# Expert outputs scattered to a row per token and choice, and read back by plain transfers

## The chip, the cores and the metric

One core of a Trainium2 chip. TensorE (PE) multiplies and transposes, VectorE (DVE) and ScalarE (ACT) read its results, GpSimd (POOL) does elementwise work and issues indirect transfers, SyncE (SP) issues the plain ones. Every engine runs its own list of instructions in order. The metric is the time of one execution in microseconds, median of several; lower is better.

## The reference

Input x is 64 x 64 x 128 (4096 tokens of 128 floats). Six residual layers follow: a gated delta rule, self and cross attention with their feed-forward parts, a block of attention and a mixture of experts, a causal attention, a mixture over eight ensembles, and a last mixture of experts. The change concerns the two mixtures in which each token goes to its two best experts of eight. Cut to what matters (the first is called f here, the last g):

```python
logits = tok @ gate_w.T + gate_b                      # f; g has no bias
topv, topi = jax.lax.top_k(softmax(logits), 2)
topv = topv / jnp.sum(topv, axis=-1, keepdims=True)
combine = zeros.at[arange(n_tok)[:, None], topi].set(topv)
for e in range(8):
    h = relu(tok @ w1[e].T + b1[e]) @ w2[e].T + b2[e]
    moe_out = moe_out + combine[:, e:e + 1] * h
x = layernorm(tok + moe_out)                          # f only; g adds moe_out to x
```

## The kernel before

The tokens are held as 16 groups of 256. A first phase ("one") does the first three layers group by group and is not touched. The second phase ("last") does the rest. In it four programs per engine (slots 0 to 3, each with a quarter of the groups and of the tiles) are woven into one list by a written string of digits, `ORDER["last"][engine]`: each digit says which program goes on to its next `yield`. Further digits stand for side programs: on POOL 4 and 5 are the `posts`, 6 to 9 the fetches; on SP 0 to 3 load expert weights, 4 to 7 store results, 8 and above do the rest. A `wait_ge` on a semaphore stops its whole engine, since the list is in order.

A mixture of experts goes like this, once for f and once for g, in two halves of tokens (f: 16 and 16 columns of 128 tokens, g: 20 and 12):

- `dve_route` and `pe_inv` sort the (token, choice) pairs by expert into tiles of 128 rows. There is room for 78 tiles in f and 78 in g (32 columns x 2 choices = 64 full tiles, and 7 more per half, since each expert's last tile may be part empty). Their results are POS (for each token and choice: its row among the tiles), EID (each tile's expert) and INV (each tile's 128 tokens), the last written in line 1994 after a copy in line 1992.
- `pool_fetch` gathers a tile's 128 rows of 512 bytes by an indirect transfer (line 2011), four buffers per slot.
- `pe_tiles` turns the tile, multiplies it by the first expert matrix (line 2122) and, after ScalarE's relu (line 2157), by the second (line 2143). `dve_tiles` adds the bias into one of two buffers wy of the slot (line 2180, signal `t_y`).
- `sp_stores` stores wy as it is, tile after tile, by a plain transfer to `yf` or `ys` in HBM (line 2095, signal `l_y`). wy is free again when that store has landed.
- `pool_got`, called by `pool_post0` (f) and `pool_post1` (g), waits until the last eight tiles of all that it reads have landed, then gathers for a group of 256 tokens the two results of each: four indirect transfers of 128 rows (line 1750) into one of two buffers GOT. `dve_two` adds them to the tokens, four instructions (line 1728, signal `q_two`), and GOT is free for the group after the next.
- In f a norm follows (`dve_post0`, POOL lines 651, 1777 and 1779, signal `q_x`) and then the causal attention, the ensembles and g's gate (`attn1`, `xattn1`, `pre1`), whose programs need POOL in lines 651 (power), 1514 (masked keys) and 2240. In g the result is stored (`sp_out`, line 2338) and the program ends.

Between f and the causal attention the tokens change their layout; `sp_back` reads the tokens, gates and positions back from HBM in the new one, and POSb holds the positions. The table WX serves f's second matrices, and then the ensembles: line 2326 loads it anew after f's last tile.

## Time and profile before

| | |
|---|---|
| time, median of 3 (lowest to highest) | 2222.42 us (2219.38 to 2223.92) |
| the profiled execution | 2224.8 us, its span 2222.9 us |
| PE, DVE, ACT, POOL busy | 86%, 70%, 55%, 43% of the span |
| f's tiles | about 1290 to 1555 us |
| attention, ensembles, g's gate | about 1555 to 2015 us |
| g's tiles | about 1995 to 2183 us |
| end | 2183 to 2222.9 us |

The span is from the first to the last instruction. "Idle before" is how long an engine stood still before the instructions of a group, and the name behind the arrow is what it waited for last. "Issue" means that it waited for nothing that the profile shows.

### The profile page before, as it was taken

To read this page: it belongs to the slowest core of one execution; us is meant where nothing else is said; L and a number is where in the kernel's file an instruction comes from. 1 tells how busy PE (TensorE), PEld (TensorE's weight loads), DVE (VectorE), ACT (ScalarE), POOL (GpSimd) and SP (SyncE) were. 2 spreads that over 40 slices of the span, in tenths; PEclk is the share of its full clock that TensorE was granted. 3 is DMA by queue.
4 is the path that set the end of the run, shared out by engine and by line. 5 is a ranking of instruction groups with operands and counts; after the bars stand their busy time and mean duration, and the time that the engine had idled before them with its cause. 6 is when DMAs were issued, how large, how long until landed. Compare 5 with 4: busy or idle time off the path is not lost.

```text
span 2222.9 us, 67944 instructions
## 1 busy us (share of the span) xinstructions
PE 1911.7 (86%) x27216; PEld 1571.6 (71%) x27216; DVE 1554.9 (70%) x4301; ACT 1211.9 (55%) x2811; POOL 961.7 (43%) x1176
## 2 busy tenths in 40 slices
PE   6789888989988998899979689787598999899992
PEld 4666676767767776677757478677377888789991
DVE  7488678787878877789757844684588766865332
ACT  6356775577765785557756345243244554344551
POOL 3542336423354234542244454250777422125466
PEclk9999999999999999999999799999599999999996
DMA  4000000000000000000010044577111010006883
GB/s 147 5 6 2 1 2 6 6 1 2 2 6 5 2 2 2 5 5 2 1 39 9 13 115 111 148 191 187 61 30 29 9 46 4 9 16 189 236 227 112
DMA packets 98342, 110.71 MB, mean 50 GB/s; under 512 B 32048, under 2 KB 72496, under 8 KB 97520
## 3 DMA queue, kind: packets, MB, share of 16 engines
q1 hardware_dynamic: 88944, 87.73, 14.1%
q0 software_dynamic: 9088, 18.63, 3.4%
q8 instruction: 221, 3.62, 0.7%
q14 instruction: 89, 0.73, 0.1%
HBM read 89.73 MB, written 16.58 MB: 48 GB/s over the span
## 4 chain that ended last, share of the span: by engine, by line
PE 58%; DVE 18%; ACT 9%; issue 7%; POOL 6%; DMA 2%; SPq 0%; POOLq 0%; DVEq 0%; ACTq 0%
PE PS L2143 6%; PE PS L2122 5%; PE PS L685 4%; PE PS L1592 4%; PE PS L1598 4%; PE PS L1071 3%; POOL GOT L1750 3%; PE PS L1086 2%; PE PS L1047 2%; DVE mx L1065 2%; PE PS L1171 2%; PE PS L1188 2%; PE PS L1060 2%; PE PS L1078 2%; PE PS L1150 2%
## 5 line engine op out<-in xcount | busy, mean ns | idle before, releaser
L2157 ACT ACTIVATE wh<-PS,we 128x128 f32<-128x128 f32 x624 | 173.3, 380 | 198.9 <-PE PS L2122 198.5
L2011 POOL DMA_INDIRECT wx<-x,INV x156 | 153.2, 982 | 150.8 <-PE PS L2134 54.6
L651 POOL TENSOR_TENSOR xrs<-xrs,Cs 128x2 f32<-128x2 f32 x112 | 78.9, 704 | 318.5 <-DVE xrs L643 317.3
L1065 DVE TENSOR_REDUCE mx<-PS 128x8 f32<-128x512 f32 x256 | 175.1, 684 | 57.1 <-PE PS L1047 28.6
L2122 PE MATMUL PS<-wxT,we 128*128 128x128 f32 x1248 | 168.9, 282 | 18.6 <-issue 14.6
L1067 DVE TENSOR_TENSOR P<-PS,mx 128x512 f32<-128x512 f32 x256 | 177.1, 692 | 8.8
L1514 POOL TENSOR_TENSOR km<-qk,Cs 128x1024 f32<-128x1024 f32 x64 | 121.2, 1901 | 129.9 <-ACT qk L1471 56.1
L1071 PE MATMUL PS<-Cs,P 128*128 128x128 f32 x1024 | 156.0, 284 | 18.7 <-ACT P L1229 12.4
L2122 PEld LDWEIGHTS PS<-wxT,we 128*128 128x128 f32 x1248 | 154.7, 196 | 24.0 <-issue 22.4
L1628 ACT ACTIVATE eh<-PS 128x256 f32<-128x256 f32 x256 | 93.6, 383 | 134.1 <-PE PS L1592 132.5
L1592 PE MATMUL PS<-exF,WX 128*128 128x256 f32 x512 | 150.5, 395 | 10.8 <-DVE X L1648 6.4
L1071 PEld LDWEIGHTS PS<-Cs,P 128*128 128x128 f32 x1024 | 117.8, 144 | 47.6 <-ACT P L1229 19.9
L1598 PE MATMUL PS<-WX,eh 128*128 128x128 f32 x1024 | 134.2, 276 | 0.1
L1598 PEld LDWEIGHTS PS<-WX,eh 128*128 128x128 f32 x1024 | 129.3, 192 | 7.1 <-ACT eh L1628 2.3
L629 ACT ACT_TABLE_LOAD x99 | 127.0, 1283 | 1.8
L1017 POOL TENSOR_TENSOR ET<-AT,Cs 128x512 f32<-128x512 f32 x64 | 83.3, 1306 | 93.0 <-PE PS L685 92.9
L2143 PE MATMUL PS<-WX,wh 128*128 x624 | 96.9, 295 | 22.6 <-DVE wxT L2175 17.7
L2180 DVE TENSOR_TENSOR wy<-PS,we 128x128 f32<-128x128 f32 x156 | 43.0, 288 | 96.2 <-PE PS L2143 84.3
L1648 DVE SCALAR_TENSOR_TENSOR X<-PS,ggt,X 128x128 f32<-128x128 f32 x256 | 76.7, 345 | 46.2 <-PE PS L1598 45.4
L1202 ACT ACTIVATE km<-PS,Cs 128x256 f32<-128x256 f32 x256 | 108.0, 483 | 0.0
L2143 PEld LDWEIGHTS PS<-WX,wh 128*128 128x128 f32 x624 | 83.4, 202 | 30.2 <-issue 29.5
L1487 ACT ACTIVATE P<-P 128x512 f32<-128x512 f32 x128 | 78.7, 629 | 46.9 <-DVE P L1067 46.0
(356 smaller groups left out, 5132.0 us busy)
## 6 DMA issues: line engine op xcount, KB each, us to landing
we<-in_wf SPq DMA_DIRECT2D x78, 322.0 KB, 4.2
we<-in_wl SPq DMA_DIRECT2D x78, 322.0 KB, 4.0
yf<-wy SPq DMA_DIRECT2D x78, 64.0 KB
ys<-wy SPq DMA_DIRECT2D x78, 64.0 KB
R<-in_wa SPq DMA_DIRECT2D x1, 3072.0 KB, 15.5
wx<-x,INV POOLq DMA_INDIRECT x156, 3.6
X<-in_x SPq DMA_DIRECT2D x4, 512.0 KB, 15.2
WX<-in_wf SPq DMA_DIRECT2D x1, 2048.0 KB, 7.8
```

The costliest lines, as they stand in the source:

```text
L629: e.preload_act_table_set(name)
L1065: e.tensor_reduce(A.mx[r], S3, AX, ALU.max).then_inc(*o.inc())
L1067: return e.tensor_tensor(v3(dst, NA), S3, bc(A.mx[r], 2, 64), ALU.subtract)
L1071: i = e.transpose(dst[:, 128 * k:128 * k + 128], P[:, 128 * k:128 * k + 128], ID)
L1202: i = e.activation(km[:, :, j, :], v3(ps(s, r)[:, W:2 * W], NB), ACT.Copy, scale=c("m64", j, j + 1))
L1514: e.tensor_tensor(A.km.rearrange("p (b j t) -> p b j t", b=NB, j=4), bc(v3(A.qk[:, W:2 * W], NB), 2, 4), bc(bc(c("m8", 4 * h, 4 * h + 4), ...
L1592: e.matmul(o, w1[:, x_, 128 * f:128 * f + 128], B.xF, True, True).then_inc(*sig.inc(G, "h_up", x_, f))
L1598: i = e.matmul(o[:, 128 * t:128 * t + 128], h[:, W * f + 128 * t:W * f + 128 * t + 128], w2[:, x_, f, :], f == 0, f == 1)
L2011: e.indirect_dma_start(out=WB[s].x[q // NS % NX], out_offset=None, in_=x1[k], in_offset=bass.IndirectOffsetOnAxis(ap=INV[k % NH][:, q - T0 ...
L2122: i = e.matmul(ps(s, 1)[:, 128 * f:128 * f + 128], w[:, 128 * f:128 * f + 128], B.xT, True, True)
L2143: i = e.matmul(ps(s, 0)[:, 0:128], B.h[:, 128 * f:128 * f + 128], W2[y][:, bass.ds(w2 + 128 * f, 128)], f == 0, f == 3)
L2157: i = e.activation(B.h[:, 128 * f:128 * f + 128], ps(s, 1)[:, 128 * f:128 * f + 128], ACT.Relu, bias=w[:, 512 + f:513 + f])
```

## The change

Results go to HBM already in token order, so that reading them back needs no index:

- `pool_got`, `pool_post1` and `sp_stores` go. New on POOL is `pool_scatter`, four programs (digits a to d): each tile is put by one indirect transfer to the rows of its tokens and choices. Rows of a tile that hold no token get a number beyond the table, and are left out by the bounds check.
- New on SP is `sp_got`: each group of 256 tokens is read by one plain transfer (128 partitions, two pieces of 1 KB each) into GOT. The number of GOT buffers (2) and wy buffers (2 per slot) stays.
- The destination rows DST come from `dve_route`. The second product of `pe_inv` now carries the pair's number, not the token column's; before INV stand four reads of PSUM and four short instructions, where one copy stood, and after it five more for DST (f: six), in the signal `r_dst`.
- POSb goes, and the positions are no longer sent through HBM (PG holds gates only).
- All five strings of the second phase are written anew. Its steps and their work are the same otherwise.

```diff
-            "4447944555755544449447555555444444555555444444555555444444555555444444555555444444555555",
+            "a69d9b6a6dcad7bb69acd7da886b8ca7dc88c7cb7c9dcb8a7b69a7966ba77a8dd9b9db9ad9b9c89dc7a9c6ddbb66ddccababdada",
...
-        def pool_got(e, s, G, y):
...
-            for q in range(T0[last + 1] - 2 * NS, T0[last + 1]):
-                e.wait_ge(*l_y.landed(q))
...
-                    e.indirect_dma_start(out=GOT[G % 2][:, t, k, :], out_offset=None, in_=rows,
-                                         in_offset=bass.IndirectOffsetOnAxis(ap=at, axis=0)).then_inc(*l_got.inc(G))
...
             e.wait_ge(*sig.at(k, "r_inv"))
-            e.tensor_copy(R.idf, ps(0, 1)[:, 0:TILES]).then_inc(*o.inc())
-            e.wait_ge(*o.now())
-            e.scalar_tensor_tensor(out=inv, in0=ps(0, 1)[:, TILES:2 * TILES], scalar=128.0, in1=R.idf, op0=ALU.mult, op1=ALU.add).then_inc(*sig.inc(k, "r_tok"))
+            part_, nth = ps(0, 1)[:, 0:TILES], ps(0, 1)[:, TILES:2 * TILES]
+            e.tensor_scalar(R.ji, nth, 1.0, 0.0, ALU.subtract, ALU.max)
+            e.tensor_scalar(R.jf, nth, 1.0, 0.0, ALU.subtract, ALU.max)
+            e.tensor_copy(R.idf, part_)
+            e.tensor_scalar(R.em, nth, 0.5, float(2 ** 20), ALU.is_lt, ALU.mult).then_inc(*o.inc())
...
+            e.tensor_scalar(R.oi, R.ji, 1, None, ALU.bitwise_and).then_inc(*o.inc())
...
+            e.tensor_copy(R.of, R.oi).then_inc(*o.inc())
...
+            e.tensor_tensor(R.to, R.jf, R.of, ALU.subtract).then_inc(*o.inc())
...
+            e.scalar_tensor_tensor(out=inv, in0=R.to, scalar=64.0, in1=R.idf, op0=ALU.mult, op1=ALU.add).then_inc(*sig.inc(k, "r_tok"))
...
+        def pool_scatter(e, s):
+            yield
+            for y in "fg":
+                for n_, q in enumerate(tiles_of(s, y)):
+                    k = part(q)
+                    to = yf if y == "f" else ys[k % NH]
+                    e.wait_ge(*sig.at(k, "r_dst"))
+                    e.wait_ge(*sig.at(q, "t_y"))
+                    e.indirect_dma_start(out=to, out_offset=bass.IndirectOffsetOnAxis(ap=DST[k % NH][:, q - T0[k]:q - T0[k] + 1], axis=0), in_=WB[s].y[n_ % 2],
+                                         in_offset=None, bounds_check=int(to.shape[0]) - 1, oob_is_err=False).then_inc(*l_y.inc(q))
+                    yield
...
-        def sp_stores(e, s):
+        def sp_got(e):
             yield
             for y in "fg":
-                for n_, q in enumerate(tiles_of(s, y)):
-                    e.wait_ge(*sig.at(q, "t_y"))
-                    rows = ys[part(q) % NH][place(q), :] if y == "g" else yf[128 * q:128 * q + 128, :]
-                    e.dma_start(rows, WB[s].y[n_ % 2]).then_inc(*l_y.inc(q))
+                for G in range(NG):
+                    h = half_with(G, y)
+                    first = groups_of(h, y)[0] if y == "g" else 0
+                    if G == first:
+                        last = 1 if y == "f" else NH + h
+                        for q in range(T0[last + 1] - 2 * NS, T0[last + 1]):
+                            e.wait_ge(*l_y.landed(q))
+                    if G >= 2:
+                        e.wait_ge(*sig.at(G - 2, "q_two", y))
+                    elif y == "g":
+                        e.wait_ge(*sig.at(NG - 2 + G, "q_two", "f"))
+                    rows = (yf if y == "f" else ys[h]).rearrange("(t p k) d -> p t (k d)", p=128, k=2)
+                    t = NT * (G - first)
+                    e.dma_start(GOT[G % 2].rearrange("p t k d -> p t (k d)"), rows[:, t:t + NT, :]).then_inc(*l_got.inc(G))
                     yield
```

The lists show three places. First, POOL when g's tiles begin, before (line 2011 is the fetch of a tile, wx its buffer; `tiles_dve_2` is the signal that slot 2 has a result):

```order
L2011 DMA wx_1_515<-x,INV_66 128x128 [waits route_dve_0,turned_pe_1]
L651 TENSOR_TENSOR ers_481<-ers_481,Cs 128x2 [waits two_dve_1]
L651 TENSOR_TENSOR ers_495<-ers_495,Cs 128x2 [waits two_dve_3]
L2011 DMA wx_2_523<-x,INV_66 128x128 [waits route_dve_0,turned_pe_2]
L2011 DMA wx_2_524<-x,INV_66 128x128 [waits route_dve_0,turned_pe_2]
L2011 DMA wx_3_533<-x,INV_66 128x128 [waits route_dve_0,turned_pe_3]
L2011 DMA wx_2_525<-x,INV_66 128x128 [waits route_dve_0,turned_pe_2]
L2011 DMA wx_0_504<-x,INV_66 128x128 [waits route_dve_0,turned_pe_0]
```

and after (line 2003 is the fetch, line 2017 the scatter of a result wy):

```order
L2003 DMA wx_1_540<-x,INV_68 128x128 [waits route_dve_0,turned_pe_1]
L651 TENSOR_TENSOR ers_506<-ers_506,Cs 128x2 [waits two_dve_1]
L2017 DMA ys<-wy_2_553,DST_66 5120x128 [waits tiles_dve_2,route_dve_0]
L2003 DMA wx_0_529<-x,INV_68 128x128 [waits route_dve_0,turned_pe_0]
L2017 DMA ys<-wy_2_554,DST_66 5120x128 [waits tiles_dve_2,route_dve_0]
L2003 DMA wx_0_530<-x,INV_68 128x128 [waits route_dve_0,turned_pe_0]
L651 TENSOR_TENSOR ers_520<-ers_520,Cs 128x2 [waits two_dve_3]
L2003 DMA wx_2_547<-x,INV_68 128x128 [waits route_dve_0,turned_pe_2]
```

Scatters stand between the fetches, each waiting for its slot's result. Behind the row of ers_520 follow 137 rows to the end of the list, all of them fetches or scatters; from g's first fetch to the end there are 158 rows: 156 indirect transfers and the two power rows.

Second, POOL near the end of its list, before (the last gathers of g's first half, POS_60, and the first of its second, POS_61, four for each group, after the tiles' results have landed, `l_y`):

```order
L1750 DMA GOT_384<-ys,POS_60 128x128 [waits l_y2,l_y1,l_y3,l_y0,l_y4,l_y7,post1_dve_0,l_y6,l_y5]
L1750 DMA GOT_384<-ys,POS_60 128x128 x3
L1750 DMA GOT_385<-ys,POS_60 128x128 [waits l_y2,l_y1,l_y3,l_y0,l_y4,l_y7,post1_dve_1,l_y6,l_y5]
L1750 DMA GOT_385<-ys,POS_60 128x128 x3
L1750 DMA GOT_384<-ys,POS_61 128x128 [waits l_y1,l_y0,l_y2,l_y7,l_y3,l_y6,post1_dve_0,l_y5,l_y4]
L1750 DMA GOT_384<-ys,POS_61 128x128 x3
L1750 DMA GOT_385<-ys,POS_61 128x128 [waits l_y1,l_y0,l_y2,l_y7,l_y3,l_y6,post1_dve_1,l_y5,l_y4]
L1750 DMA GOT_385<-ys,POS_61 128x128 x3
```

and after (fetches into wx, scatters from wy):

```order
L2017 DMA ys<-wy_1_543,DST_67 3072x128 [waits tiles_dve_1,route_dve_0]
L2003 DMA wx_0_528<-x,INV_69 128x128 [waits route_dve_0,turned_pe_0]
L2003 DMA wx_0_529<-x,INV_69 128x128 [waits route_dve_0,turned_pe_0]
L2017 DMA ys<-wy_3_563,DST_67 3072x128 [waits tiles_dve_3,route_dve_0]
L2017 DMA ys<-wy_3_564,DST_67 3072x128 [waits tiles_dve_3,route_dve_0]
L2017 DMA ys<-wy_2_553,DST_67 3072x128 [waits tiles_dve_2,route_dve_0]
L2017 DMA ys<-wy_2_554,DST_67 3072x128 [waits tiles_dve_2,route_dve_0]
L2017 DMA ys<-wy_0_534,DST_67 3072x128 [waits tiles_dve_0,route_dve_0]
L2017 DMA ys<-wy_1_544,DST_67 3072x128 [waits tiles_dve_1,route_dve_0]
L2017 DMA ys<-wy_0_533,DST_67 3072x128 [waits tiles_dve_0,route_dve_0]
```

Five more scatters end the list. The 24 gathers of g's last six groups are gone from it, and six reads on SP stand in their place.

Third, SP when f's tiles end, before (line 2095 stores a result, line 2326 loads the ensembles' table):

```order
L2095 DMA yf<-wy_3_538 128x128 [waits tiles_dve_3]
L2095 DMA yf<-wy_1_519 128x128 [waits tiles_dve_1]
L2095 DMA yf<-wy_2_528 128x128 [waits tiles_dve_2]
L2095 DMA yf<-wy_0_509 128x128 [waits tiles_dve_0]
L2326 DMA WX<-in_wx 128x4096 [waits tiles_pe_0,tiles_pe_1,tiles_pe_3,tiles_pe_2]
L2063 DMA x<-gzq_540 128x2x128 [waits two_dve_0]
L2063 DMA x<-gzq_541 128x2x128 [waits two_dve_1]
```

and after (line 2109 reads a group's results, `post0_dve` is the signal of `dve_two` and the steps behind it):

```order
L2109 DMA GOT_409<-yf 128x2x256 [waits l_y2,l_y3,l_y1,l_y4,l_y0,l_y5,l_y7,l_y6]
L2109 DMA GOT_410<-yf 128x2x256
L2109 DMA GOT_409<-yf 128x2x256 [waits post0_dve_0]
L2109 DMA GOT_410<-yf 128x2x256 [waits post0_dve_1]
L2109 DMA GOT_409<-yf 128x2x256 [waits post0_dve_0]
L2109 DMA GOT_410<-yf 128x2x256 [waits post0_dve_1]
L2336 DMA WX<-in_wx 128x4096 [waits tiles_pe_0,tiles_pe_1,tiles_pe_3,tiles_pe_2]
```

The stores have moved to POOL; the table's load, which came right after them, now comes behind the reads of six groups, the last two of which wait for groups 2 and 3 to be added.

## Rows read from the trace of the kernel before

**Rows 1.** The page: busy time, share of the span and instructions of each engine.

```profile
PE 1911.7 (86%) x27216; PEld 1571.6 (71%) x27216; DVE 1554.9 (70%) x4301; ACT 1211.9 (55%) x2811; POOL 961.7 (43%) x1176
```

**Rows 2.** Windows: us; PE, PEld, DVE, ACT, POOL busy; granted clock; DMA share; GB/s.

```profile
1445.00:1555.00 110.00, 90.11 (x695) 84.54 (x695) 73.15 (x129) 46.30 (x168) 38.22 (x38) 0.94 0.79 190
1555.00:1575.00 20.00, 0.00 (x0) 0.00 (x0) 7.43 (x28) 0.00 (x0) 13.98 (x16) 0.54 0.41 142
1575.00:1610.00 35.00, 28.06 (x246) 17.41 (x246) 23.96 (x60) 12.60 (x25) 27.98 (x26) 0.53 0.06 16
1610.00:1750.00 140.00, 128.14 (x1332) 105.12 (x1329) 119.12 (x387) 63.36 (x157) 103.98 (x111) 1.00 0.10 27
...
1995.00:2183.00 188.00, 176.41 (x1505) 169.69 (x1502) 74.24 (x284) 92.39 (x330) 113.45 (x118) 1.00 0.75 209
2183.00:2222.90 39.90, 0.00 (x0) 0.00 (x0) 9.66 (x32) 0.00 (x0) 25.00 (x27) 0.52 0.31 85
```

**Rows 3.** Chain that ended last, 1540 to 1760 us: shares by line.

```profile
by line: POOL GOT L1750 18.2%; issue 11.9%; PE PS L1592 6.5%; PE PS L1598 5.8%; DVE X L1728 5.1%; PE PS L1060 3.9%; PE PS L1071 3.7%; PE PS L1086 3.6%; PE PS L2143 2.8%; POOL X L1777 2.7%; POOL km L1514 2.6%; DVE X L647 2.5%; PE PS L2122 2.
```

**Rows 4.** Timeline of POOL as f's results are read: start, us, instruction, idle before.

```profile
1557.25 0.95 POOL L1750 DMA_INDIRECT GOT<-yf,POSb  x1 [50.17 <-DMA yf<-wy]
```

**Rows 5.** Timeline of DVE there.

```profile
1552.46 0.88 DVE L2180 TENSOR_TENSOR wy<-PS,we 128x128 f32<-128x128 f32 x4 [5.26 <-PE PS L2143]
1563.74 1.27 DVE L1728 SCALAR_TENSOR_TENSOR X<-GOT,PGb,X 128x128 f32<-128x128 f32 x4 [10.40 <-DMA GOT<-yf,POSb]
...
1568.77 2.10 DVE L1728 SCALAR_TENSOR_TENSOR X<-GOT,PGb,X 128x128 f32<-128x128 f32 x4 [0.29 <-DMA GOT<-yf,POSb]
...
1581.68 1.25 DVE L1728 SCALAR_TENSOR_TENSOR X<-GOT,PGb,X 128x128 f32<-128x128 f32 x4
...
1591.19 1.26 DVE L1728 SCALAR_TENSOR_TENSOR X<-GOT,PGb,X 128x128 f32<-128x128 f32 x4
...
1617.10 1.27 DVE L1728 SCALAR_TENSOR_TENSOR X<-GOT,PGb,X 128x128 f32<-128x128 f32 x4
```

**Rows 6.** Timeline of POOL at the end.

```profile
2213.72 0.95 POOL L1750 DMA_INDIRECT GOT<-ys,POS  x1 [0.30 <-issue]
2214.98 0.95 POOL L1750 DMA_INDIRECT GOT<-ys,POS  x1 [0.30 <-issue]
```

**Rows 7.** Timeline of DVE at the end: last result, last two groups added.

```profile
2179.95 0.29 DVE L2180 TENSOR_TENSOR wy<-PS,we 128x128 f32<-128x128 f32 x1 [0.52 <-PE PS L2143]
...
2212.47 1.26 DVE L1728 SCALAR_TENSOR_TENSOR X<-GOT,GK,X 128x128 f32<-128x128 f32 x4 [3.75 <-DMA GOT<-ys,POS]
2217.51 1.26 DVE L1728 SCALAR_TENSOR_TENSOR X<-GOT,GK,X 128x128 f32<-128x128 f32 x4 [3.78 <-DMA GOT<-ys,POS]
```

**Rows 8.** DMA issues of the page: KB each, median us from issue to landing.

```profile
we<-in_wf SPq DMA_DIRECT2D x78, 322.0 KB, 4.2
...
x<-X SPq DMA_DIRECT2D x16, 128.0 KB, 1.8
...
WX<-in_wx SPq DMA_DIRECT2D x1, 2048.0 KB, 8.1
```

**Rows 9.** Line 1592, the ensembles' first product: ns, first and last start us.

```profile
L1592 PE MATMUL PS<-exF,WX x512: 379/379/483, 1623.7 to 2015.2; 128*128 128x256 f32 x171
```

**Rows 10.** Timeline of DVE as INV of g's first half is written.

```profile
1995.94 0.21 DVE L1992 COPY ridfk<-PS 128x47 f32<-128x47 f32 x1 [2.64 <-PE PS L1860]
1996.19 0.21 DVE L1994 SCALAR_TENSOR_TENSOR INV<-PS,ridfk 128x47 int32<-128x47 f32 x1
```

**Rows 11.** Timeline of POOL where g's fetches begin.

```profile
1997.16 1.05 POOL L2011 DMA_INDIRECT wx<-x,INV  x1 [5.53 <-DVE INV L1994]
1998.51 0.95 POOL L2011 DMA_INDIRECT wx<-x,INV  x1 [0.30 <-issue]
```

**Rows 12.** Line 2095, the stores: ns min/median/max to issue one, first and last start us.

```profile
L2095 SPq DMA_DIRECT2D ys<-wy x78: 319/432/1314, 2007.8 to 2180.3; - x78
```

**Rows 13.** Tile wx: ns min/median/max, first and last start us; issue to landing.

```profile
L2011 POOL DMA_INDIRECT wx<-x,INV x156: 942/953/1482, 1288.6 to 2158.5; - x156
...
DMA to landing us min/median/max: 2.4/3.6/5.9
```

**Rows 14.** Tile GOT: ns min/median/max of one, first and last start us.

```profile
L1750 POOL DMA_INDIRECT GOT<-yf,POSb x64: 943/976/1191, 1557.3 to 1731.4; - x64
...
L1750 POOL DMA_INDIRECT GOT<-ys,POS x64: 951/955/1084, 2124.5 to 2215.0; - x64
```

**Rows 15.** Groups of POOL by line: shapes, count | busy us, mean ns | idle before.

```profile
L651 POOL TENSOR_TENSOR ers<-ers,Cs 128x2 f32<-128x2 f32 x48 | 34.1, 711 | 119.7 <-DVE ers L643 119.0
```

**Rows 16.** Windows of line 2180 alone: us, busy (x results), clock, DMA share, GB/s.

```profile
1995.00:2183.00 188.00, 21.92 (x78) 1.00 0.75 209
1445.00:1555.00 110.00, 10.74 (x42) 0.94 0.79 190
```

**Rows 17.** Windows of line 2011 alone, the same columns.

```profile
1995.00:2183.00 188.00, 75.51 (x78) 1.00 0.75 209
1445.00:1555.00 110.00, 38.22 (x38) 0.94 0.79 190
```

168 lines of the change are left out of this document (80 added, 88 removed).

## The prediction

> **What bounds the kernel now.** I read the page's busy times first [rows 1]: PE works 86% of the span, so what the change can give lies where PE stands still or waits. The windows [rows 2] show where that is in the second phase. PE is idle in the whole of 1555 to 1575 us, between f's tiles and the causal attention, and works 28.06 of 35 us up to 1610 and 128.14 of 140 us up to 1750. In g's tiles it works 176.41 of 188 us, and after 2183 us, for 39.9 us, not at all. From 1555 to 1610 the granted clock is 0.53 to 0.54: PE has just stood still, and most of that stretch is at the lower of the two levels, 1.2 GHz; from 1610 on it is 1.00, 2.4 GHz.
>
> The chain of waits over 1540 to 1760 us [rows 3] then names the cause of the first hole: the gathers of line 1750 have 18.2% of it, 40 of 220 us, more than any other line. The timelines of POOL and DVE give the steps: the first gather goes out at 1557.25 [rows 4], DVE can add the first group only at 1563.74, when four gathers have landed, and later groups follow at 1568.77, 1581.68, 1591.19 and 1617.10 [rows 5], since the gathers share POOL with powers and key masks.
>
> At the end POOL issues gathers back to back, 0.95 us each and 0.30 us between them, so one in 1.26 us [rows 6]. A group takes four, 5.04 us, and DVE adds the groups at just that pace: 2212.47, 2217.51, waiting 3.75 us each time [rows 7]. So the last 40 us are paced by POOL's gathers, while SP has nothing to do but to store. From the last addition (2217.51 + 1.26) to the end of the span are 4.1 us.
>
> **The change part by part.**
>
> *Turn from f to attention.* Removed: 64 gathers from POOL, some 64 x 1.26 = 81 us of its list from 1557 to 1732 [rows 14]. POOL was busy 27.98 of 35 and 103.98 of 140 us there [rows 2]. Added: before the first read the last scatters must land. The last four results come together at 1552.46 to 1553.34 [rows 5], so four scatters queue on POOL, 4 x 1.26 = 5.0 us, and the last lands 2.5 us after its issue (the last gather goes out at 2214.98 and DVE starts on it at 2217.51 [rows 6, 7]): 1552.7 + 3.8 + 2.5 = 1559.0, where the store had landed by 1557.25, when POOL's wait for it ended [rows 4]. Then one plain read of 256 KB on SP. None is in the trace. The nearest rows are a store of 128 KB at 1.8 us and a load of 322 KB at 4.2 us, the latter beside other loads [rows 8]; I take 3.0 us, between them, with 0.4 us to issue it, and keep 1.8 and 4.2 as ends. DVE starts at 1562.4 instead of 1563.7: 1 us. The rest comes from the groups behind the first two. Each now waits only for its buffer and 3.4 us of read, so by this reading group 1 can come some 4 us earlier (near 1564.5, behind group 0), group 2 some 10 us (1563.7 + 3.4 + 1.3 at the earliest, 1570 with DVE's norms between), and group 3 more. What that is worth is bounded by PE's holes: 35 - 28.06 + 140 - 128.14 = 18.8 us above, nothing below, since DVE works 119.12 of 140 us there too and would be late next. I take 8 us, a little under the middle, because of DVE. The load of the ensembles' table, 8.1 us [rows 8], now stands behind the reads of groups 2 and 3, which wait until groups 0 and 1 are added, by about 1568. It lands by some 1577, and line 1592 first needs it at 1623.7 [rows 9]: nothing, with 46 us of cover.
>
> *Routing.* INV now stands behind four reads of PSUM and four dependent short instructions instead of one copy and one instruction. A dependent pair is 0.25 us apart (1995.94 to 1996.19 [rows 10]), the reads overlap: 3 more steps and 3 more reads, 1.2 us. It lies on the way to the first fetch, for which POOL waited 5.53 us at g's start [rows 11], and once more in f's second half. I count 2 us for both. The five or six instructions for DST come behind INV, 1.3 us of DVE in a half, hidden by the time until a tile has a result.
>
> *g's tiles.* The stores leave SP, where an issue took 0.43 us [rows 12], and 78 scatters join 78 fetches on POOL. The step from one fetch to the next is 1.25 us (1998.51 - 1997.16, less the first one's extra [rows 11]; median 0.953 [rows 13] and 0.30). A scatter is not in the trace: another direction, and rows left out by the bounds check. Nearest is the gather: 0.94 to 1.19 us in f [rows 14], and the fetch's longest, 1.48 us [rows 13]. Below: 78 x 128 = 9984 places hold 8192 pairs, so 18% are left out, and if time goes by rows written, 0.78 us. I take 0.953, as for a fetch. Then from g's first fetch POOL has 156 x 1.255 + 2 x 0.71 [rows 15] = 197 us of work, against 188 us that g's tiles take now [rows 2], with 78 results and 78 fetches [rows 16, 17]. POOL becomes what sets the end of g's tiles: 1997.2 + 197 = 2194.4 without a gap. The list is in order, and a scatter holds the fetches behind it until its result is there; four fetch buffers and two result buffers per slot soften that. I take 3 us of gaps. The last scatter then starts at 2196.4 and lands at 2199.
>
> *The end.* The six groups of g's second half remain. Two buffers make three rounds of 0.4 + 3.0 + 1.3 = 4.7 us, and 1.3 us for the second of the last pair: 15.4 us; with 4.1 us for the last store the span ends 19.5 us after the landing, at 2218.5. Before it was 2222.9. So 39.9 us of tail become about 20, and 15 of the 20 us gained go to POOL's longer list before it.
>
> *Sum.* 2218.5 - 8 (turn) + 2 (routing) = 2212.5 of span. The profiled execution was 2224.8, 1.9 us above its span, and 2.4 above the median of the runs: 2212.5 + 1.9 - 2.4 = 2212 us, 10.4 us or 0.5% less. In f's last 110 us there are 42 results and 38 fetches, 80 x 1.255 = 100 us of POOL [rows 16, 17]: it fits, barely, and I add nothing.
>
> The Trainium skill has a rule against this. In the fetches' rows the median is 953 ns beside a DVE at work, and the longest 1482 ns [rows 13]. The page SBUF — State Buffer, section SBUF: two separate sides, says that a DMA issued from GpSimd cannot write its descriptors while DVE runs a copy in a two-port mode, and gives 620 ns alone against 3100 ns overlapped, which plain issues from SP escape. By that a scatter would be as dear as DVE's copies make it, at worst 2.1 us more each; by the rows it is 0.5 us more in the rarest case. I go by the rows. It is the mechanism behind the dear scatter below.
>
> **The rivals.**
>
> *Cheap scatters.* Rows left out shorten them to 0.78 us. For it: a gather's time should go by its rows. Against: no row shows a shorter list. POOL's work falls by 78 x 0.17 = 13 us, and 2212 - 13 = 2199 us. PE's own pace would allow no more than some 5 us beyond that.
>
> *Dear scatters, slower.* A write to HBM by indices with a bounds check costs more on POOL than a gather. Place: POOL's list in g's tiles, which has no slack. Price: 78 times the excess, so from 0.13 us each the 10.4 us are gone. At 1.19 us [rows 14] it is 78 x 0.24 = 19 us: 2231. At 1.48 us it is 41 us, and 42 x 0.53 - 10 = 12 us in f: 2265. For it: nothing in the trace bears on the check; against: all 284 indirect transfers have medians of 0.95 to 0.98 us.
>
> *Lists that hold each other up, about no change.* A scatter waiting for its result holds fetches, PE waits for those, and SP's read of g's first half, which waits for the landing, holds the loads of expert weights behind it. With 12 us of gaps instead of 3: 2221. The same time comes out if attention after the turn is held by DVE and not by the gathers: 2212 + 8 = 2220. For it: POOL would be fully occupied in order, DVE nearly so at 1610 to 1750.
>
> **How the numbers follow.** Forecast 0.42, cheap scatters 0.15, dear scatters 0.20, held-up lists 0.23. Of the last 0.05 are faster, 0.12 the same, 0.06 slower. Same means within 0.2%, 4.4 us, which is about what a measurement of this kernel can tell. Faster: 0.42 + 0.15 + 0.05 = 0.62; same 0.12; slower 0.26. The likeliest case has its own range of 2204 to 2218 (turn worth 2 to 14, read 1.8 to 4.2 us in three rounds). The whole range runs from cheap scatters with a good turn, 2195, to dear ones at 1.19 us and a read of 4.2, 2236.
>
> **What would show it.** Right: after the change POOL's rows in g's tiles follow each other 1.25 us apart with few waits over 3 us, its busy time there is near 150 us, PE waits for wx or its results wait to be scattered; DVE's last additions come in pairs, under 5 us from pair to pair; the last result to the end is some 25 to 35 us; between 1575 and 1750 PE has fewer than 18 us of holes. Wrong: a scatter's mean is off 0.95 us by more than 0.1; POOL is idle for over 15 us in g's tiles; the plain read takes over 4.2 us; or the attention's start hasn't moved while DVE is busy throughout.

## The result, and the profile after

The changed kernel takes 2246.69 us (median of 4, 2243.8 to 2250.36) against 2221.43 beside it: ratio 1.0104, interval 1.0079 to 1.0128. It is slower; 2212 was predicted, outside its range of 2195 to 2236. The profiled execution has a span of 2245.6 us, 33.1 more than the 2212.5 that the sum gave.

Where things stand in the two traces (start of the instruction, us; fetches of wx, results wy, additions from GOT; the end is that of the span):

| kernel | first fetch f | first result f | last result f | first addition f | first fetch g | last result g | end |
|---|---|---|---|---|---|---|---|
| before | 1288.6 | 1305.7 | 1553.1 | 1563.7 | 1997.2 | 2179.9 | 2222.9 |
| after | 1299.9 | 1329.4 | 1596.1 | 1604.2 | 2022.8 | 2225.4 | 2245.6 |

By this the tail is as forecast: from g's last result to the end 20.2 us, where it was 43.0. Everything ahead of it is late: 43 us at f's last result, 25.6 at g's first fetch (so the turn and the attention gave 17.4 back), 45.5 at g's last result.

The page's busy times after, against [rows 1]:

```profile
PE 1930.5 (86%) x27216; PEld 1588.7 (71%) x27216; DVE 1550.0 (69%) x4342; ACT 1210.0 (54%) x2811; POOL 994.7 (44%) x1204
```

Windows of the trace after (us; PE, PEld, DVE, ACT, POOL busy; granted clock; DMA share; GB/s):

```profile
1250.00:1350.00 100.00, 70.64 (x791) 58.94 (x791) 52.44 (x132) 35.37 (x86) 43.19 (x39) 0.77 0.23 50
...
1450.00:1600.00 150.00, 107.98 (x830) 101.65 (x828) 98.17 (x203) 52.00 (x189) 90.70 (x88) 0.86 0.70 166
1600.00:1650.00 50.00, 24.88 (x304) 17.24 (x305) 37.80 (x120) 15.03 (x31) 27.29 (x30) 0.69 0.26 85
1650.00:1750.00 100.00, 98.38 (x998) 83.12 (x999) 89.29 (x310) 47.73 (x123) 44.03 (x51) 1.00 0.09 27
2045.00:2205.00 160.00, 142.40 (x1186) 133.60 (x1185) 58.45 (x230) 76.63 (x279) 122.42 (x124) 1.00 0.71 201
```

The holes of PE that the gathers left behind the turn [rows 2] are nearly gone: it is busy 98.38 of 100 us from 1650 on. The prediction had named 1575 to 1750 us for this, with 18.8 us of holes before; the same stretch 43 us later has 9. The turn itself stays, with 24.88 of 50 us. But PE stands still for 42 of the 150 us in which f's second half runs, and in g's tiles it has 142 of 160. In that last row POOL has 124 instructions in 160 us, one in 1.29; 60 fetches and 63 scatters are issued there, and 0.30 us stand between two. The timeline of POOL shows a piece of it, fetches and scatters in turn, and the last scatter of all, which stood 0.95 us, the longest wait between two of POOL's instructions in g's tiles:

```profile
2099.41 0.97 POOL L2003 DMA_INDIRECT wx<-x,INV  x1 [0.30 <-issue]
2100.69 1.01 POOL L2017 DMA_INDIRECT ys<-wy,DST  x1 [0.30 <-issue]
2102.01 0.97 POOL L2003 DMA_INDIRECT wx<-x,INV  x1 [0.30 <-PE PS L2148]
2103.28 1.18 POOL L2017 DMA_INDIRECT ys<-wy,DST  x1 [0.30 <-issue]
...
2226.78 0.98 POOL L2017 DMA_INDIRECT ys<-wy,DST  x1 [0.95 <-issue]
```

The scatter by its line (ns min/median/max of one, first and last start), and the plain read's issue, answer to [rows 13] and [rows 14]:

```profile
L2017 POOL DMA_INDIRECT yf<-wy,DST x78: 967/996/2136, 1330.5 to 1599.1; - x78
L2017 POOL DMA_INDIRECT ys<-wy,DST x78: 980/1002/1184, 2042.3 to 2226.8; - x78
L2109 SPq DMA_DIRECT2D GOT<-ys x16: 359/382/540, 2184.9 to 2239.1; - x16
```

The timeline of DVE at the end answers to [rows 7]: the last result, an addition that was due, and then the last six groups, in pairs 4.0 and 4.1 us apart:

```profile
2225.36 0.29 DVE L2194 TENSOR_TENSOR wy<-PS,we 128x128 f32<-128x128 f32 x1 [1.49 <-PE PS L2157]
2225.56 1.25 DVE L1728 SCALAR_TENSOR_TENSOR X<-GOT,GK,X 128x128 f32<-128x128 f32 x4
2232.04 2.44 DVE L1728 SCALAR_TENSOR_TENSOR X<-GOT,GK,X 128x128 f32<-128x128 f32 x8 [5.22 <-DMA GOT<-ys]
2236.05 1.26 DVE L1728 SCALAR_TENSOR_TENSOR X<-GOT,GK,X 128x128 f32<-128x128 f32 x4 [1.57 <-DMA GOT<-ys]
2237.78 1.26 DVE L1728 SCALAR_TENSOR_TENSOR X<-GOT,GK,X 128x128 f32<-128x128 f32 x4 [0.47 <-DMA GOT<-ys]
2240.17 1.26 DVE L1728 SCALAR_TENSOR_TENSOR X<-GOT,GK,X 128x128 f32<-128x128 f32 x4 [1.12 <-DMA GOT<-ys]
2242.12 1.26 DVE L1728 SCALAR_TENSOR_TENSOR X<-GOT,GK,X 128x128 f32<-128x128 f32 x4 [0.69 <-DMA GOT<-ys]
```

SP's part of it, each pair of plain reads; the additions of 2232.04, 2236.05 and 2240.17 start 2.7 to 2.8 us behind the first issue of their pair:

```profile
2229.30 0.88 SPq L2109 DMA_DIRECT2D GOT<-ys  x2
...
2233.33 1.53 SPq L2109 DMA_DIRECT2D GOT<-ys  x2
...
2237.34 2.10 SPq L2109 DMA_DIRECT2D GOT<-ys  x2
```

The start of f is where the first 24 us go. POOL's list of after has the first fetch right behind the key masks, and it waits 33.69 us for INV; PE goes on with attention, and its first expert product comes at 1319.00, the first result at 1329.36 (timelines of DVE, POOL, PE, and last POOL's first fetch in the trace of before, with a wait of 10.68 us):

```profile
1299.38 0.20 DVE L1967 SCALAR_TENSOR_TENSOR INV<-rtok,ridfk 128x39 int32<-128x39 f32 x1
1299.88 1.23 POOL L2003 DMA_INDIRECT wx<-x,INV  x1 [33.69 <-DVE INV L1967]
1319.00 1.22 PE L2136 MATMUL PS<-wxT,we 128*128 128x128 f32 x4 [1.72 <-DVE wxT L2184]
1329.36 0.49 DVE L2194 TENSOR_TENSOR wy<-PS,we 128x128 f32<-128x128 f32 x2 [1.03 <-PE PS L2157]
...
1288.58 1.22 POOL L2011 DMA_INDIRECT wx<-x,INV  x1 [10.68 <-DVE INV L1994]
```

From INV to the first result are 30.0 us, where 17.6 were.

### The profile page after: what moved, and what is told of

Same layout as the page of the kernel before. It is cut to its first block, busy times and chain, and to the rows that moved or that the text cites. A ratio compares the mean times of both kernels' runs of the same rounds, so it can differ in the third digit from the quotient of the medians.

```text
span 2245.6 us, 68082 instructions
## 1 busy us (share of the span) xinstructions
PE 1930.5 (86%) x27216; PEld 1588.7 (71%) x27216; DVE 1550.0 (69%) x4342; ACT 1210.0 (54%) x2811; POOL 994.7 (44%) x1204
## 4 chain that ended last, share of the span: by engine, by line
PE 58%; DVE 19%; ACT 9%; issue 7%; POOL 4%; DMA 3%; SPq 0%; POOLq 0%; DVEq 0%; ACTq 0%
PE PS L2157 5%; PE PS L1592 4%; PE PS L1598 4%; PE PS L685 4%; PE PS L2136 4%; PE PS L1071 3%; DVE mx L1065 2%; PE PS L1086 2%; DVE P L1067 2%; PE PS L1047 2%; PE PS L1171 2%; PE PS L1060 2%; PE PS L1150 2%; PE PS L1078 2%; PE PS L1188 2%
## 5 line engine op out<-in xcount | busy, mean ns | idle before, releaser
L2136 PEld LDWEIGHTS PS<-wxT,we 128*128 128x128 f32 x1248 | 158.6, 201 | 24.7 <-issue 18.8
```

The lines of the kernel that those rows point to most:

```text
L2136: i = e.matmul(ps(s, 1)[:, 128 * f:128 * f + 128], w[:, 128 * f:128 * f + 128], B.xT, True, True)
```

## The experiments

Two theories stood after this reading. A: the scatters in POOL's in-order list slow the tiles, whatever the order. B: the five strings, which were laid anew, cost the time by themselves. To part them, one kernel took over the other's order: every step of a program keeps its place in the other's string, and a step that the other doesn't have (a scatter, a read) is put where that kernel's trace shows its input ready.

### Transfers and order apart

Run 1: the changed kernel, order of before. The first piece of POOL's string (a to d are the scatters):

```diff
-            "1100122330233120111100002332222311100110122233003111220123332222333231110001077998886698677611788189ccc1181c998
+            "abcd1133220013013220111100002223332311111100022233111003122023332223332000011131998877978889996600088cdc11898d
```

> The changed kernel's transfers (scatters on POOL, plain reads on SP, the longer routing) in the order of the kernel before: PE and ACT as they stood there, on DVE, POOL and SP each added step put where the trace of before shows its input ready (a scatter about 1 us behind its result, a read where the group's gathers began). Theory A, the scatters in POOL's in-order list slow the tiles whatever the order is: 2240 to 2255 us, the time of the changed kernel. Theory B, the orders laid anew cost the time (INV 11 us later, f's tiles 20 us slower): 2205 to 2222 us. Between them, 2225 to 2238, both have a share. The last result comes by 2185 by B, after 2205 by A; from it to the end about 20 us by both.

Run 2: stores and gathers, order of after. The gathers are a program of their own:

```diff
+        def pool_gots(e):
+            for y in "fg":
+                for G in range(NG):
+                    yield from pool_got(e, 0, G, y)
```

> The mirror image: stores on SP, four gathers a group on POOL and the short routing, in the order of the changed kernel; stores stand 0.3 us behind their result, the gathers where the plain reads stood, as a program of their own. Theory A: 2215 to 2228 us, the time of before, as the scatters are gone. Theory B: 2240 to 2265 us, as the order is kept and the tail of 40 us is back; the first result stays near 1329.

Run 3: order of after, plain stores of SP in place of the scatters. They put the results in the order of the tiles, so the reads that follow take rows of other tokens; their number and size are the same. Run 4: the same in the order of before.

```diff
-                    e.indirect_dma_start(out=to, out_offset=..., in_=WB[s].y[n_ % 2], ...).then_inc(*l_y.inc(q))   # POOL
+                    e.dma_start(to[r:r + 128, :], WB[s].y[n_ % 2]).then_inc(*l_y.inc(q))                           # SP
```

> The changed kernel with its order, but each scatter is taken from POOL and a plain store of the same 64 KB from SP stands in its place (the results land in the order of the tiles, so the output is not the reference's; reads, DST and all else stay). Prices what the scatters cost on POOL and as transfers. Theory A: 2200 to 2218 us, all of the loss and more comes back. Theory B: 2235 to 2247 us, since the order stays.

> As the run before with plain stores from SP in place of the scatters, but in the order of the kernel before. What the plain reads and the longer routing give without any price for the scatters: by both theories 2195 to 2208 us (before, less 20 us of tail, less some of the turn, plus 2 of routing). Against the first run of this set it prices the scatters in the old order: A says 35 us or more, B under 12.

Measured, beside 2219.55 us for the kernel before on that chip:

| run | median us | ratio (interval) | first result f | last result f | first fetch g | last result g | end |
|---|---|---|---|---|---|---|---|
| 1 scatters, old order | 2239.04 | 1.0083 (1.0056 to 1.011) | 1308.9 | 1573.0 | 2007.2 | 2214.5 | 2236.8 |
| 2 gathers, new order | 2355.71 | 1.0605 (1.0562 to 1.0648) | 1330.8 | 1593.7 | 2080.4 | 2321.1 | 2361.9 |
| 3 stores, new order | 2249.9 | 1.0134 (1.0089 to 1.0179) | 1328.7 | 1594.3 | 2018.4 | 2230.4 | 2249.0 |
| 4 stores, old order | 2201.9 | 0.99 (0.9867 to 0.9933) | 1312.2 | 1570.6 | 1999.3 | 2179.4 | 2202.3 |

Neither theory holds alone. Run 1 falls 1 us under A's window and 1 over the one that gave both a share, run 3 3 us over B's; run 4 is inside its own. In the old order the scatters cost 37 us (1 against 4), as A says; in the new one nothing that can be seen (3 against after, ratios 1.0134 and 1.0104), and there the order costs 48 us without any scatter (3 against 4), as B says. So two limits stand side by side, each enough for most of the loss, and taking one away alone gains little. The windows of g's tiles show the two, in the order runs 1, 4, 3:

```profile
2020.00:2180.00 160.00, 134.93 (x1101) 130.44 (x1100) 55.35 (x219) 68.88 (x249) 122.00 (x124) 0.94 0.66 185
```

```profile
2010.00:2170.00 160.00, 152.94 (x1320) 148.22 (x1318) 65.39 (x259) 82.31 (x297) 68.47 (x72) 1.00 0.82 227
```

```profile
2045.00:2205.00 160.00, 138.12 (x1123) 129.84 (x1122) 52.63 (x206) 71.59 (x261) 56.65 (x59) 0.97 0.72 196
```

Run 1 has POOL full with 124 instructions, as after has; run 4 has 72 and PE at 152.94; run 3 has 59, POOL idle for two thirds, and PE still only at 138.12. There POOL isn't the limit, and what differs from run 4 is the order. Which of the five strings holds the tiles is not shown.

Run 2 came 90 us above even B's window. Its chain of waits from 1600 to 1790 us starts with the gathers, a quarter of 190 us (shares by line, cut at the right as the view cuts it):

```profile
by line: POOL GOT L1750 25.2%; issue 14.6%; DVE X L1728 7.5%; PE PS L1598 5.2%; PE PS L1592 4.0%; DVE X L1648 3.6%; POOL km L1514 3.0%; POOL X L1775 2.7%; PE PS L1071 2.1%; POOL X L1777 2.0%; DVE nz L647 2.0%; DVE mx L1065 2.0%; POOL po0rs 
```

From the last result of f to g's first fetch it takes 487 us, after takes 427: by the chain, an order that calls for additions at the pace of plain reads makes DVE stand for gathers. So its time says nothing of the order's own cost, for which I had made it. The part ahead of the gathers does. It has neither scatters nor the longer routing, and yet its first result comes 31.0 us behind INV and its last result of f at 1593.7; run 3 has 29.9 us and 1594.3, after 30.0 and 1596.1. In the old order the first result comes 16.1 to 17.8 us behind INV (runs 1, 4, 5 and before). The late start of f is the order's.

### How the parts add up

Run 5: as run 4, with INV as before and no DST.

```diff
-            ...  e.scalar_tensor_tensor(out=inv, in0=R.to, scalar=64.0, in1=R.idf, ...)   and DST
+            e.tensor_copy(R.idf, ps(0, 1)[:, 0:TILES]).then_inc(*o.inc())
+            e.wait_ge(*o.now())
+            e.scalar_tensor_tensor(out=inv, in0=ps(0, 1)[:, TILES:2 * TILES], scalar=128.0, in1=R.idf, ...)
```

> The run with plain stores in the order of before (2202 us), now also with the routing of before: INV from one copy and one instruction, no DST (it isn't used there). In that run f's tiles lagged the kernel before by 12 us, 8 of them at the second half's INV, and the attention after the turn made it up again. If the longer routing is the cause of the lag, f's last result comes within 5 us of before's 1553 and the time is 2186 to 2196 us. Rival, the routing is worth its own 1 us a half and the rest is how the core drifts (clock, DMA): 2198 to 2205 us.

Runs 6 and 7 join the two orders at the turn; each engine's string is the one order's prefix and then the other's remaining steps:

```diff
+ORDER["last"][k] = steps of one order begun by 1612 (7: 1640) us + the other order without them
```

> The changed kernel, all its transfers, in the order of before up to the turn (all steps begun by 1612 us of the run in the old order) and in the changed order from there. By adding up stretches: first fetch of g at 2007 as in the old order, then the changed order's 223 us to the end: span 2230, 2228 to 2236 us. Rival, the changed order pays in g what it saves in waits of POOL only with its own f before it: 2237 to 2247. If all the loss of the changed order were in f: 2222.

> The mirror image: the changed order up to the turn (steps begun by 1640 us), the order of before from there. Adding up: first fetch of g at 2023, then 230 us: span 2253, 2248 to 2258 us. If the two orders' costs don't add (the attention between absorbs f's lateness), 2235 to 2245.

Run 8: run 1, with every second scatter of g taken to SP.

```diff
+                    if y == "g" and n_ % 2:     # pool_scatter; sp_stores has these
+                        yield
+                        continue
```

> The changed kernel's transfers in the order of before (2239 us), but every second result of a slot in g is stored by SP instead of scattered, 39 of 78 or so, and the reads of g read the rows of f's results, so the output is not the reference's. If POOL's list is a capacity (156 transfers of 1.295 us against tiles that need 172 to 181 us), 117 of them take 152 us and hide: the time falls nearly all the way, 2202 to 2212 us. If each scatter costs its share, by its wait in the list or as a transfer, half of 37 us comes back: 2217 to 2224 us.

Measured on another chip, beside 2224.15 us for the kernel before:

| run | median us | ratio (interval) | first result f | last result f | first fetch g | last result g | end |
|---|---|---|---|---|---|---|---|
| 5 short routing | 2198.74 | 0.9892 (0.9858 to 0.9925) | 1307.4 | 1560.1 | 1992.4 | 2175.9 | 2198.7 |
| 6 old f, new g | 2238.29 | 1.0063 (1.0043 to 1.0082) | 1308.7 | 1571.0 | 2006.5 | 2209.4 | 2229.6 |
| 7 new f, old g | 2250.52 | 1.0121 (1.0086 to 1.0156) | 1327.9 | 1592.1 | 2023.3 | 2232.3 | 2254.4 |
| 8 half of g's scatters | 2206.85 | 0.9939 (0.9911 to 0.9967) | 1309.4 | 1569.8 | 2000.3 | 2181.0 | 2204.1 |

Run 8 is the plainest. Taking 38 of 156 transfers away gives 32 of the 37 us back, not half, and g's last result comes at 2181.0, as without any scatter (2179.4). POOL's list is a capacity: 118 x 1.295 = 153 us fit under the 180 that the tiles take, 156 x 1.295 = 202 don't. A rival would be that a result's buffer comes free later, since a scatter must land first. DVE does wait 19.8 us for landed scatters in run 1's g, but in run 8, where more than half of the results still go by scatter, 1.4 us. So that wait comes with the full list. The window of run 8's g, against run 4's:

```profile
2010.00:2170.00 160.00, 152.82 (x1316) 148.16 (x1316) 65.80 (x258) 82.22 (x297) 104.62 (x108) 1.00 0.79 224
```

The traces of runs 6 and 7 came as added up from stretches (2230 and 2253 of span; 2229.6 and 2254.4): the new order costs 16 us by g's first fetch, and with scatters it is 7 us better than the old in g itself (223.1 against 229.6 us from first fetch to end). The medians say less. The profiled execution of run 6 is the fastest of its 7, that of run 7 the slowest of its 4, and run 6's median of 2238.29 lies in the window of its rival, 2237 to 2247. By the ratios the new order up to the turn costs 0.4% (run 7 against 1, after against 6), some 8 to 9 us both times, and in g it gains 0.2% (6 against 1), which their intervals don't tell from nothing.

Run 5's time doesn't bear out the routing as a cause: its median differs from run 4's by 3 us, its ratio by 0.0008, and 2198.74 lies in the window of the rival (2198 to 2205), not in the one of the longer routing (2186 to 2196). The bound on f's last result, within 5 us of 1553, was missed by 2. The traces show more: f's last result is 10.5 us earlier than in run 4, g's first fetch 6.9. And in every trace of the old order on such chips the second INV of f follows the first by 150.6 to 154.3 us with the short routing (before, runs 5 and 19), by 160.2 to 164.5 with the long one (runs 1, 4, 6 and 8). So the delay inside f is there; how much of it reaches the end isn't settled.

### Each half alone

Run 9 cuts the two orders at 1300 us instead of the turn; runs 11 and 12 have the change in g alone and in f alone, in the order of before (each with the other half's stores, gathers and routing as they were).

```diff
-            for y in "fg":      # pool_scatter, sp_got; the long routing, DST
+            for y in "g":       # run 11; run 12: "f"
```

> The changed kernel, in the order of before only for the steps begun by 1300 us (routing of f's first half, INV at 1293), and in the changed order from there. By the traces the changed order loses 7 us before INV and 14 us between INV and the first result of f (1299.6 to 1329.6, against 1293.0 to 1309.2). If the 14 us lie in the order behind the cut, the first result stays 28 to 31 us behind INV, near 1323, and the time is 2238 to 2244 us. If they come from what stood before it (key masks and routing mixed otherwise), the first result follows 16 to 18 us behind INV and the time is 2230 to 2236.

> Half of the change alone, in the order of before: f keeps stores on SP, gathers on POOL and the short routing; g has scatters, plain reads and the long routing. First fetch of g within 3 us of before's 1997, then the 230 us that the run in the old order took for g: 2224 to 2232 us, 3 to 9 more than before. If g's transfers paid after all without f's disturbance, under 2216.

> The other half alone, in the order of before: f has scatters, plain reads and the long routing, g is as before. First fetch of g near 2007 by the run in the old order, then before's 226 us: 2228 to 2236 us. If f's lateness of 10 us there was drift of those runs (5 us of it stood in phase one), 2218 to 2226. Faster than before, under 2214, only if the turn's gain of some 16 us outlives the routing and the scatters.

These ran where the kernel before takes 2349.72 us, and so did the three again, with a trace of the kernel before (run 13), and 11 and 12 a third time; only the last run met a time of before like the first. I call the two the fast and the slow kind of chip, though what makes the difference isn't known: the record gives the number 10 both to the chip of runs 13 to 16 and to that of run 19. Times of the two kinds aren't compared, only ratios. These are the record's; the quotient of two medians differs from them by up to 0.3%.

> The kernel before, for a trace from the same chip as the next three: 2218 to 2226 us if the chip is like the first, near 2350 if it is like the one of the last set.

> The kernel with the change in g alone, a second time. On a chip where before takes 2221: first fetch of g near 1997, g 226 to 230 us, 2221 to 2230 us. The ratio of the last set was 0.9991.

> The kernel with the change in f alone, a second time. If f's half costs by itself what the ratio 1.0103 of the last set says, 2236 to 2246 us with g's first fetch 15 to 22 us late; by the stretches of the run in the old order (g's first fetch at 2007) 2228 to 2236.

> The order of before up to 1300 us and the changed one behind it, a second time. As said before: first result near 1323 and 2238 to 2244 us if the 14 us between INV and the first result lie in the order behind the cut; 2230 to 2236 if in what stood before it. The ratio of the last set, 1.0229, says worse than both: 2260 or more.

> The change in g alone. On a chip where before takes 2221 us, POOL's 156 transfers (202 us) are longer than g's tiles (183 us): capacity theory 2224 to 2232 us, ratio 1.001 to 1.005, last result of g near 2205 and the end 20 us behind it. If POOL is no bound: 2200 to 2212, ratio under 0.996. On a chip where before takes 2352 the theory says 0.996 to 1.000, as twice before.

> The change in f alone. On a chip where before takes 2221 us: f's last result 15 to 20 us late, 7 to 10 left at g's first fetch, g as before: 2228 to 2236 us, ratio 1.003 to 1.007. On a chip where before takes 2352: 1.008 to 1.012, as twice before.

> The change in g alone once more. On a chip where before takes 2221 us: 2224 to 2232 us by the capacity theory, 2200 to 2212 if POOL is no bound. On one where it takes 2352: 2344 to 2352, as before.

| kernel | before there | ratios | traces: first fetch g, last result g, end |
|---|---|---|---|
| before (13) | 2352 | | 2051.1, 2315.5, 2355.1 |
| g alone (11, 14, 17) | 2350 to 2352 | 0.9991 (0.9968 to 1.0014), 0.9977 (0.9959 to 0.9995), 0.9983 (0.9959 to 1.0007) | 2040.1, 2314.9, 2337.0 (14) |
| f alone (12, 15, 18) | 2350 to 2352 | 1.0103, 1.0096, 1.0104 | 2066.3, 2329.3, 2368.8 (15) |
| cut at 1300 (9, 16) | 2350 to 2352 | 1.0229, 1.0191 | 2080.6, 2378.2, 2398.4 (16) |
| g alone (19) | 2225.46 | 1.0032 (1.0014 to 1.005) | 1996.7, 2205.6, 2229.2 |

The change in g alone costs 0.3% on the fast kind, as the capacity said ahead of run 19 (2224 to 2232), and on the slow kind it is 0.1 to 0.2% under before, in one of three timings beyond its interval. Where g's tiles take 183 us, POOL's 202 set the pace, and run 19's window shows it full; where they take 264 of themselves, it isn't (run 14):

```profile
2010.00:2170.00 160.00, 134.88 (x1084) 130.70 (x1083) 54.09 (x216) 67.59 (x246) 122.06 (x124) 0.93 0.65 183
```

```profile
2075.00:2235.00 160.00, 117.72 (x849) 112.09 (x849) 40.04 (x159) 52.18 (x192) 98.48 (x99) 0.86 0.52 142
```

The traces give both sides of the sum, from g's first fetch to its last result and from there to the end. On the fast kind the tiles take 208.9 us in place of 182.7, and the tail is 19.4 us shorter (run 19 against before). On the slow kind they take 273.0 to 280.3 (runs 11, 14 and 17) in place of 263.0 to 267.5 (runs 12, 13, 15 and 18), and the tail is 16 to 18 us shorter (against run 13). So the capacity explains why the cost falls, but not that 6 to 17 us of it are left, though POOL stands still for 73 us of run 14's 276, beyond the 0.30 us between two. No run shows what these are.

The change in f alone costs 1% there, more than the 0.3 to 0.7% that I had from the stretches. Against run 13, run 15 is 35.6 us late at f's last result and 15.2 at g's first fetch; beside the run of g alone of the same set, whose f is that of before, they are 45 to 49 and 26 to 31 (runs 12, 15, 18 against 11, 14, 17). POOL's 202 us fit easily into the 300 us and more of f there, so this isn't the capacity, and no run shows what it is. On the fast kind it wasn't timed. There the runs with the whole change in the old order have their first fetch of g at 2000.3 to 2007.2 (8, 6 and 1) against 1997.2, so it would cost 3 to 10 us by then. Runs 9 and 16, the cut at 1300, came at 1.0229 and 1.0191, far over both windows (1.004 to 1.010). With INV written in the old order, their first result came 40 to 41 us behind the first fetch, where runs 11 to 15, 17 and 18 have 29.7 to 32.4. So some 8 to 11 us lie in the order behind the cut. That its end is 43 us later than run 13's, more than any of the joined orders on the fast kind, is not explained.

On the fast kind no version with whole scatters or gathers (after, runs 1, 2, 6, 7 and 19) beat the kernel before. A shorter list for POOL with an order made for it might; that wasn't tried.

## Why the prediction was wrong

The sum missed by 33.1 us. By its own steps:

| step | forecast us | measured us | off |
|---|---|---|---|
| first fetch of g (turn -8, routing +2, f's tiles 0) | 1991.2 | 2022.8 | +31.6 |
| from there to the last scatter's start | 199.2 | 204.0 | +4.8 |
| from there to the end | 22.1 | 18.8 | -3.3 |

*The failed step* is the zero for f and for the new strings. The sum takes f over at its old pace with the words "it fits, barely, and I add nothing", and has no term for the order of the steps. The reason that it gives, POOL's capacity, held: in the old order f's last result came at 1573.0, 1571.0 and 1569.8 us with scatters (runs 1, 6, 8) and at 1570.6 without (run 4). What it left out is that all five strings were laid anew. Last result of f and first fetch of g, us:

| | stores, short routing | stores, long routing | scatters, long routing |
|---|---|---|---|
| old order | 1560.1, 1992.4 (run 5) | 1570.6, 1999.3 (run 4) | 1569.8 to 1573.0, 2000.3 to 2007.2 (runs 1, 6, 8) |
| new order | 1593.7 (run 2, whose gathers then hold g back) | 1594.3, 2018.4 (run 3) | 1592.1 to 1596.1, 2022.8 to 2023.3 (after, run 7) |

By g's first fetch the new order costs 19.1 us without scatters and 15.6 to 23.0 with them, in place of 0. Along one path through the table, before 1997.2, run 5 1992.4, run 4 1999.3, run 1 2007.2, after 2022.8, the 31.6 us split so: the turn gave 4.8 (8.0, if one takes off the 3.2 us by which run 5's first fetch is late already) where I took 8; routing cost 6.9 in place of 2; f's scatters 7.9 in place of 0; the order 15.6. The scatters' share is the least sure: by run 8, whose f is that of run 1, it is 1.0. These differences of single traces are good to some 3 us each at best, and phase one alone, which no edit touches, moves by up to 5. In g the new order gives part of its cost back: at the end after is 8.8 us of span and 7.7 of median over run 1.

The order isn't all of the miss. In the old order the same transfers have a span of 2236.8 us (run 1), 24.3 over the sum: 16.0 by g's first fetch, 9.6 more to the last scatter, 1.3 less behind it. Its median of 2239.04 would have been outside the range too. The gain was judged well: plain reads alone, with neither scatters nor longer routing, bring the span to 2198.7 (run 5), 24.2 us less, where the sum has 28. What was too small is what the change costs in return: 38.1 us in the old order (run 1 against 5), 46.9 in the new, where the sum has 17.

*Routing.* I priced the instructions ahead of INV, 1.2 us a half, and hid DST. The instructions ahead of INV did cost about that: from the first read of PE's product to INV are 1.4 us in after, 0.44 in before. But the delay grew: in the old order f's second INV follows the first 6 to 14 us later than with the short routing, and in the new order nothing is seen of it (runs 2 and 3 in the table). Where f's second half gets its INV, PE waits 2.96 us for DVE in run 4 and then 3.72 more; at the same product before (last row) it waits 0.54. That the one follows from the other is my reading, not shown:

```profile
1467.34 1.22 PE L2155 MATMUL PS<-WX,wh 128*128 x4 [2.96 <-DVE wxT L2187]
...
1475.27 0.45 PE L2146 MATMUL PS<-Cs,wx 128*128 128x128 f32 x1 [3.72 <-DVE wy L2192]
...
1453.02 1.22 PE L2143 MATMUL PS<-WX,wh 128*128 x4 [0.54 <-DVE wxT L2175]
```

The clock falls there in both. The windows of that stretch, run 4 and then before (us, engines' busy time, granted clock, DMA share, GB/s):

```profile
1462.00:1467.00 5.00, 0.96 (x7) 0.58 (x5) 0.29 (x2) 0.00 (x0) 3.78 (x4) 0.88 0.63 108
1467.00:1474.00 7.00, 4.21 (x18) 3.92 (x18) 6.76 (x8) 2.18 (x8) 5.17 (x5) 0.50 0.53 106
1474.00:1480.00 6.00, 4.73 (x25) 4.76 (x26) 5.34 (x9) 0.00 (x0) 4.08 (x5) 0.54 0.52 138
1480.00:1486.00 6.00, 5.44 (x49) 5.25 (x48) 4.67 (x9) 4.36 (x16) 0.94 (x1) 1.00 0.65 164
```

```profile
1440.00:1450.00 10.00, 5.97 (x64) 5.19 (x62) 8.47 (x13) 2.18 (x8) 5.34 (x6) 0.86 0.87 148
1450.00:1455.00 5.00, 4.24 (x18) 3.87 (x19) 2.58 (x4) 0.00 (x0) 3.92 (x4) 0.50 0.86 113
1455.00:1460.00 5.00, 4.35 (x27) 4.05 (x27) 4.50 (x8) 2.18 (x8) 3.79 (x4) 0.75 0.63 166
1460.00:1465.00 5.00, 4.43 (x40) 4.25 (x39) 4.29 (x9) 3.01 (x12) 3.94 (x4) 1.00 0.66 192
```

At two levels, 1.2 and 2.4 GHz, a mean of 0.50 is 1.2 throughout: 10.3 us of the lower one in before's rows (2.8 + 5 + 2.5), 13.7 in run 4's (1.2 + 7 + 5.5). Ahead of the fall PE had stood still for 4.03 of 10 us in before and for 4.04 of 5 in run 4. So run 4 has 3.4 us more of the lower clock, at half speed 1.7 us of work.

*g's tiles.* Right in mechanism, short in size. POOL did become the bound. Its step is 1.295 us and not 1.255 (the scatter is 1.00, the fetch 0.97, not 0.953): the list is 156.2 us of work where the sum has 150.1. Between the instructions stand 48.8 us in all, where it has 50.1 (156 x 0.302, and 3 of gaps). In the old order the same stretch takes 208.8 and 210.2 us (runs 1 and 19), 10 to 11 over the forecast of 199.2, so that the new order hid half of this miss.

*The end.* Right, and 3 us better: the pairs are 4.0 and 4.1 us apart, 4.7 was the forecast, and from issue to addition are 2.7 to 2.8 us, for which I had 3.4. Only the sign that I had named was off: from the last result to the end I expected 25 to 35 us, as for a POOL that lags behind its results, and it is 20.2; the last scatter starts 1.4 us behind the last result, so in place of a backlog the tiles themselves were held.

*The rivals.* Cheap scatters fell: the shortest of all 156 takes 0.967 us, though 18% of the places hold no token. Dear scatters fell as worded: the excess over 0.953 is 0.05 us each in g and 0.08 in f, where 0.13 would have eaten the gain. The Trainium skill (page SBUF — State Buffer, section SBUF: two separate sides) says that a DMA issued from GpSimd is held up while DVE runs a copy in a two-port mode, and gives 3100 ns for one so overlapped, 620 alone. Here f's 78 scatters average 1.03 us and the longest is 2.14, 1.2 over a fetch's median: an excess of that size doesn't occur in the trace, a smaller one at most now and then. The held-up lists fit no better: the 12 us of gaps that they put in g's list aren't there, since POOL never waits more than 0.95 us, and f's last result came no later with scatters than without.

*The order.* I had read the new strings at two or three places and taken them as the same steps moved a little. The chance that a new order costs as much as the whole change may bring stood in no rival. That and the costs above are what made the range too low.

## What to carry to other kernels

Count an in-order engine's transfers against the stretch that must hide them, with the gap between two as part of the price. Here 118 in 180 us cost next to nothing (run 8 against 4) and 156, which take 202, stretched g's tiles to 207 (run 1). The count is a lower bound and not the whole cost: on the slow kind of chip 156 fitted into 264 us and g's tiles still took 6 to 17 us more. And the same edit can pay where the tiles are slower and cost where they are faster. When a change comes with a schedule laid anew, time the two apart: keep the old order and put in only the new steps. Removing one limit can gain nothing while the schedule laid around it stands, as taking the scatters out of the new order did (run 3). And a term of zero needs its reason checked against everything that the edit touches: the reason for f, POOL's capacity, was right, and the new order was not in it.

## What the runs showed of the hardware

- An indirect scatter of 128 rows of 512 bytes with a bounds check takes POOL 1.00 us and 0.30 us to the next, a fetch 0.97 (medians of after; 0.953 for a fetch in before). A scatter lands 3.5 to 3.7 us after its issue in the median, of the 39 whose landing the trace of after gives, and a fetch 3.7. 18% of the places of all scatters lie beyond the bounds, and still none of the 156 takes less than 0.967 us.
- A plain read of 256 KB in pieces of 1 KB is issued by SP in 0.36 to 0.44 us (medians of after and run 1). In run 1 it lands 2.5 to 5.0 us after its issue in f, median 2.9, and 2.8 to 6.9 in g, median 3.6.
- Two levels of time for one program: the kernel before took 2219.55 to 2225.46 us in four sets of runs, 2349.72 to 2352.16 in three. Single instructions take as long as ever in the slow ones (a product of 128 columns 275 ns in the median in both), and the first INV comes within a few us of its usual time (1283.0 to 1295.3 us). What is slower are the tiles: g's 264 us against 183, f's 310 against 264, from first fetch to last result. In run 13 DVE waits 58.4 us, 12 times, before results and ACT 123.6 us, 18 times, before its part of the tiles for something that the profile calls remote, which the trace of before doesn't have. What it is stays open, and so does whether it belongs to the chip: the chip number 10 has both levels (runs 13 to 16, and 19).
